# A fused four-stage kernel on one Trainium2 core: block 2's local sums taken out of the head into group 0, and each deferred block's x1 loaded in one piece

## The chip, the cores and the metric

The kernel runs on 1 core of one Trainium2 chip. The metric is the device time of the whole program in microseconds (us), lower is better. Before the change it is 701.6 us, the median of 3 runs (700.96 to 702.64). Instructions of five engines run side by side and wait for each other on semaphores: PE (TensorE), DVE (VectorE), ACT (ScalarE), POOL (GpSimd) and SP (SyncE, which here only issues DMAs).

## The reference

`x` has shape 2 x 2048 x 512 (two sequences, f32). Four residual stages follow each other:

```
x = x + L0(x)   # per sequence: scores from tanh(x W1 + b1) v, masked softmax over all positions, pooled sum / count
x = x + L1(x)   # stencil: zX*(left + right - 2y) along channels + zY*(row before + row after - 2y) + zR*y*(1-y)
x = x + L2(x)   # adapter: LayerNorm(y + relu(y Wd + bd) Wu + bu), weights picked by profile id
x = x + L3(x)   # recurrent mixer: causal EMAs (scans over time), gates (Wg, Wn1, Wtemp, Wsoma), Wout, LayerNorm
```

The output of L0's stage is called x1 below, that of L1's stage x2, that of L2's stage x3. For the stencil stage the kernel splits x2 of a block of rows into local sums (x1*(mid - zR*x1), and zX times the left and right channel neighbours), which need that block alone, and the rows before and after it, scaled by zY, which are added by DMA from a copy in DRAM (`beside_scratch`).

## The kernel before, in words

The 4096 rows are 32 chunks of 128 rows; 4 chunks make a block (512 rows), and there are 8 blocks, 0 to 3 in the first sequence, 4 to 7 in the second. Each engine has one instruction stream, written out by hand; every wait is a semaphore wait in that stream, and what stands behind it on the engine waits too.

**The head** (up to about 139 us) computes L0. PE alternates the score matmuls (L1030, L1043, L1050), the sums, the transposes of the probabilities (L1086, L1099) and `pooled(b, c)` (L1125, L1126), one chunk of x1 each; DVE finishes a chunk in `x1(b, c)` (L1513), which also frees the PSUM bank that a later `pooled` writes. Between these, PE does the adapter of block 0: `x2_transposes(0)` (L1164), `down(0)` (L1174), `up(0)` (L1184), and DVE and ACT its LayerNorm. Blocks 0 to HEAD_BLOCKS-1 = 2 get their local sums here, over whole blocks of 128 x 2048: ACT `mix_local(n)` (L742), DVE `by_local(n)` (L1519), POOL `channels(n)` (L574 to L577, into `side`, which lies in `xts[2]`), DVE `stencil(n)` (L1526). ACT `scale_beside(n)` (L756) writes zY*x1 of each block, in place for the head's blocks and into one of three `xts` slots for the others; SP `store_beside(n)` (L410) writes it to DRAM, `store_x1(n)` (L419) writes x1 of blocks 3 to 7 to `x1_scratch`. POOL then adds to x2 in place by DMAs: `add_up_bias(q)` and `add_shift(q)` (L615), `add_before(q)` (L605), `add_after(q)` (L611), each 1 MB.

**The groups** g = 0 to 7 follow, one per block: PE runs `front(g)` (N1, four times 24 matmuls of gate logits with one small matmul L1224 behind the first set), `x2_transposes(g+1)`, `soma_in`, `down(g+1)`, `up(g+1)`, `temporal(g)`, `x3_transposes(g+1)` (L1193) and `output(g)`; nearly all its matmuls are at L1129 to L1131. DVE runs for each chunk k `logits` (scan, L1647), `traces` (L1655 to L1668), `blend_traces` (L1676) and `trace_lo` (L1684), then the LayerNorm of block g+1 (L1616, L1623, L1631), `product` and `product_lo` (L1690, L1697), `x3_lo(g+1)` (L1638) and `out_apply` (L1705, L1709).

The local sums of blocks 3 to 7 are **deferred**: they are made in group q-3 and early in q-2, one chunk at a time. SP `load_late(q, c)` (L429) loads a chunk of x1 into the single buffer `late_y` once the chunk before is consumed, ACT `late_mix` (L766) writes into x2, DVE `late_by_local` (L1603) and `late_stencil` (L1609), POOL `late_channels` (L584 to L588, into `late_side`). The x2 buffers of blocks 2, 4, 6 (`x2b0`) and 3, 5, 7 (`x2b1`), the traces (`th`, `tl`) and others lie over memory that the head uses, `xb` and the `xts` slots among them: an engine that first writes there waits until the stores that read it have landed (`beside_landed`). In group 0, `trace_lo(0, 0)` waits so for block 7's store.

## Time and profile before

| what | before |
|---|---|
| median of 3 runs | 701.6 us |
| the profiled execution: its own time / its span | 702.7 us / 700.7 us |
| PE busy | 666.1 us (95%) |
| DVE busy | 526.5 us (75%) |
| ACT busy | 363.3 us (52%) |
| POOL busy | 174.2 us (25%) |
| chain that ended last | PE 79%, DVE 9%, ACT 4%, DMA 4%, SP's queue 2% |
| moved by DMA | 85.77 MB, mean 122 GB/s |

Start times are microseconds from the start of the span. "Idle before <- releaser" is how long the engine stood before the instruction and whose semaphore came last. PE's busy time counts overlapping matmuls once. The granted clock of PE is given as a share of 2.4 GHz, so 0.50 is its lower level of 1.2 GHz.

### The profile page before, as it was taken

How to read it: one execution, taken by the hardware profiler on the slowest of the kernel's cores; microseconds unless marked ns; L12 is line 12 of the kernel's file. 1: busy time of each engine (PE TensorE's matmuls, PEld its weight loads, DVE VectorE, ACT ScalarE, POOL GpSimd, SP SyncE). 2: the span in 40 equal slices, each digit the busy share in tenths (PEclk: the TensorE clock that was granted, in tenths of full speed). 3: DMA queues.
4: the chain of work that ended last, by engine and by line, in shares of the span. 5: the costliest groups of instructions: out<-in, count | busy, mean ns of one | idle time of the engine just before them, and what ended most of it. 6: DMA issues, size and time to landing. Idle time of an engine off the chain costs nothing.

```text
span 700.7 us, 8057 instructions
## 1 busy us (share of the span) xinstructions
PE 666.1 (95%) x2792; PEld 484.8 (69%) x2792; DVE 526.5 (75%) x747; ACT 363.3 (52%) x745; POOL 174.2 (25%) x259
## 2 busy tenths in 40 slices
PE   4969988989999999999999999999999999999996
PEld 1535444468577868786878687868786878687875
DVE  2676789847996888589868986887689649864955
ACT  0143366582675366536653566456635653565245
POOL 5003440110044214411451235123512210111001
PEclk9989999999999999999999999999999999999998
DMA  7996998999522661465147524742465230022001
GB/s 201 326 335 222 258 203 201 359 263 322 106 36 74 150 101 29 102 135 97 30 117 129 87 35 120 131 77 39 127 93 88 38 83 1 0 48 74 0 1 60
DMA packets 51670, 85.77 MB, mean 122 GB/s; under 512 B 8480, under 2 KB 10528, under 8 KB 51630
## 3 DMA queue, kind: packets, MB, share of 16 engines
q0 software_dynamic: 16896, 33.56, 30.1%
q1 hardware_dynamic: 31230, 51.69, 20.6%
q10 hardware_dynamic: 3504, 0.01, 0.3%
q8 instruction: 22, 0.36, 0.2%
q14 instruction: 18, 0.15, 0.1%
HBM read 63.22 MB, written 22.04 MB: 122 GB/s over the span
## 4 chain that ended last, share of the span: by engine, by line
PE 79%; DVE 9%; ACT 4%; DMA 4%; SPq 2%; issue 1%; POOLq 0%; ACTq 0%; POOL 0%; DVEq 0%
PE bank L1130 20%; PE bank L1129 20%; PE bank L1131 20%; PE bank L1184 3%; PE bank L1174 3%; PE bank L1125 3%; PE bank L1030 3%; DMA beside_scratch<-xts 2%; PE bank L1164 2%; PE bank L1193 2%; DMA xts<-in_xT 1%; SPq L410 1%; DVE xb L1513 1%; DVE x2b L1519 1%; PE bank L1224 1%
## 5 line engine op out<-in xcount | busy, mean ns | idle before, releaser
L1668 DVE TENSOR_TENSOR_SCAN tr<-alpha,carry,tr 128x512 f32<-128x512 f32 x48 | 58.8, 1267 | 0.0
L1129 PE MATMUL bank<-th,wg_l 128*128 128x512 f32 x128 | 52.0, 406 | 0.0
L1129 PE MATMUL bank<-xh,wg_l 128*128 128x512 f32 x128 | 51.9, 406 | 0.0
L1130 PE MATMUL bank<-tl,wg_h 128*128 128x512 f32 x128 | 50.5, 395 | 0.0
L1130 PE MATMUL bank<-xl,wg_h 128*128 128x512 f32 x128 | 50.5, 395 | 0.0
L1131 PE MATMUL bank<-th,wg_h 128*128 128x512 f32 x128 | 50.2, 392 | 0.0
L1131 PE MATMUL bank<-xh,wg_h 128*128 128x512 f32 x128 | 50.2, 392 | 0.0
L840 ACT ACTIVATE carry<-tr 128x2 f32<-128x2 f32 x32 | 6.6, 205 | 80.4 <-DVE tr L1668 80.3
L624 POOL TENSOR_TENSOR rs_a<-ss_a,consts 128x1 f32<-128x1 f32 x32 | 14.3, 447 | 118.7 <-ACT junk L788 118.1
L1125 PE MATMUL bank<-xb,probT 128*128 128x512 f32 x64 | 36.4, 652 | 5.5 <-DVE xb L1513 5.4
L1655 DVE SCALAR_TENSOR_TENSOR wgb<-wgb,soma 128x512 f32<-128x512 f32 x32 | 22.2, 692 | 25.4 <-ACT wgb L834 25.4
L1647 DVE TENSOR_TENSOR_SCAN wgb<-alpha,carry,bank 128x512 f32<-128x512 f32 x24 | 30.4, 1266 | 9.8 <-PE bank L1131 9.8
L858 ACT ACTIVATE wide<-bank,bias_temp 128x512 f32<-128x512 f32 x32 | 21.8, 683 | 29.6 <-PE bank L1131 29.6
L1690 DVE SCALAR_TENSOR_TENSOR wide<-wide,soma 128x512 f32<-128x512 f32 x32 | 21.3, 685 | 18.9 <-ACT wide L858 18.9
L584 POOL TENSOR_TENSOR late_side<-late_y 128x510 f32<-128x510 f32 x20 | 21.4, 1072 | 53.7 <-DMA late_y<-x_scratch 53.6
L766 ACT ACTIVATE x2b<-late_y,coef 128x512 f32<-128x512 f32 x20 | 16.2, 810 | 35.0 <-DMA late_y<-x_scratch 35.0
L1603 DVE TENSOR_TENSOR x2b<-x2b,late_y 128x512 f32<-128x512 f32 x20 | 14.7, 736 | 25.9 <-ACT x2b L766 25.8
L1709 DVE SCALAR_TENSOR_TENSOR xr<-wgb,rs_o,xr 128x512 f32<-128x512 f32 x32 | 27.7, 864 | 6.3 <-POOL rs_o L626 4.7
L1705 DVE SCALAR_TENSOR_TENSOR wgb<-bank,nmu_o,gamma_row 128x512 f32<-128x512 f32 x32 | 23.9, 746 | 9.4 <-ACT junk L874 9.2
L1513 DVE SCALAR_TENSOR_TENSOR xb<-bank,rnorm,xb 128x512 f32<-128x512 f32 x32 | 23.0, 743 | 10.5 <-PE bank L1126 10.5
L615 POOL DMA_DIRECT2D xr<-rows_scratch x10 | 13.5, 1350 | 63.3 <-PE bank L1193 52.9
L624 POOL TENSOR_TENSOR rs_o<-ss_o,consts 128x1 f32<-128x1 f32 x32 | 8.4, 262 | 83.0 <-ACT junk L874 83.0
(264 smaller groups left out, 1995.3 us busy)
## 6 DMA issues: line engine op xcount, KB each, us to landing
x2b<-beside_scratch POOLq DMA_DIRECT2D x12, 1024.0 KB, 9.2
xr<-rows_scratch POOLq DMA_DIRECT2D x10, 1024.0 KB, 10.6
xb<-in_x SPq DMA_DIRECT2D x8, 1024.0 KB, 14.2
result<-xr SPq DMA_DIRECT2D x7, 1024.0 KB, 4.2
x2b<-rows_scratch POOLq DMA_DIRECT2D x6, 1024.0 KB, 9.5
x_scratch<-xb SPq DMA_DIRECT2D x5, 1024.0 KB, 10.5
beside_scratch<-xts SPq DMA_DIRECT2D x5, 1024.0 KB, 11.5
late_y<-x_scratch SPq DMA_DIRECT2D x20, 256.0 KB, 2.9
```

What stands on the lines that cost most here:

```text
L624: po.tensor_tensor(rs[:, c:c + 1], ss[:, c:c + 1], eps, ALU.add).then_inc(chain, 1)
L858: act.activation(wide[:, k], bank[TEMP(g)[k]][:], ACT.Tanh, bias=bias_temp[:, k:k + 1], scale=0.5).then_inc(gate_act, 1)
L1125: pe.matmul(acc, probT[:, c], xb[:, b, c], start=True, stop=False)
L1129: pe.matmul(acc, wl, xh_, start=start, stop=False)
L1130: pe.matmul(acc, wh, xl_, start=False, stop=False)
L1131: return pe.matmul(acc, wh, xh_, start=False, stop=stop)
L1513: ve.scalar_tensor_tensor(xb[:, b, c], bank[POOLED(b, c)][:], rnorm[:, b, c:c + 1], xb[:, b, c], ALU.mult, ALU.add).then_inc(x1_done, 1)
L1647: ve.tensor_tensor_scan(wgb[:, k % 2], alpha[:, 0:1].broadcast_to([P, GN]), bank[CTX[k]][:], 0.0 if first else carry[:, k, 0:1], ALU.mult, ...
L1655: ve.scalar_tensor_tensor(w, w, 1.0, x3f[:, k], ALU.add, ALU.mult).then_inc(gated, 1)
L1668: ve.tensor_tensor_scan(t[:, d], alpha[:, 1 + d:2 + d].broadcast_to([P, GN]), t[:, d], 0.0 if first else carry[:, k, 1 + d:2 + d], ALU.mul ...
L1705: ve.scalar_tensor_tensor(t, bank[OUT[c]][:], nmu_o[:, c:c + 1], gamma_row[:], ALU.add, ALU.mult).then_inc(o_w, 1)
L1709: ve.scalar_tensor_tensor(xr[:, g % 2, c], t, rs_o[:, c:c + 1], xr[:, g % 2, c], ALU.mult, ALU.add).then_inc(o_done, 1)
```

## The change

1. `HEAD_BLOCKS` is 2. `mix_local(2)`, `by_local(2)`, `stencil(2)` and `channels(2)` leave the head. Block 2 is handled as the deferred ones, chunk by chunk: chunk 0 and 1 between the end of the head and group 0's first logits, 2 and 3 within group 0. Its x1 is copied by one DMA from `xb` to `x2b0` (`keep_x1`, SBUF to SBUF), and its `beside` copy goes through an `xts` slot.
2. `load_late(q)` loads the whole block (1 MB) straight into its x2 buffer instead of four chunks into `late_y`. `late_mix` writes to a separate tile `late_mixed`, `late_by_local` multiplies in place, and must now wait for POOL's `late_channels`, which reads the same chunk.
3. The `xts` slots are used in another turn, so the waits on landed stores name earlier blocks: `trace_lo(0, 0)` waits for block 6's, not block 7's.
4. On DVE `trace_lo(g, k)` for k = 0, 1 moves behind the next chunk's `logits` and `blend_traces`; the deferred stencils of chunk 3 and chunk 2 move up a place. POOL's three adding DMAs for block 2 move into group 0.

```diff
-HEAD_BLOCKS = 3
+HEAD_BLOCKS = 2
...
-                return x1_of(n) if n < HEAD_BLOCKS else as_tiles(xts[n % 3])
+                return x1_of(n) if n < HEAD_BLOCKS else as_tiles(xts[(n - HEAD_BLOCKS) % 3])
...
+                    def keep_x1(q):
+                        sp.wait_ge(x1_done, GT * (q + 1))
+                        sp.wait_ge(beside_out[0][0], 32)
+                        sp.dma_start(x2_of(q), x1_of(q)).then_inc(late_in, 16)
...
+                    def load_late(q):
+                        sp.wait_ge(x1_out[q], 16)
+                        if q == HEAD_BLOCKS + 1:
+                            beside_landed(sp, 1, 3)
                         else:
-                            sp.wait_ge(late_v, n)
-                            sp.wait_ge(late_chan, 3 * n)
-                        sp.wait_ge(x1_out[q], 16)
-                        sp.dma_start(late_y[:], x1_rows(q)[:, c]).then_inc(late_in, 16)
+                            sp.wait_ge(x3_done, GT * (q - 1))
+                        sp.dma_start(x2_of(q), x1_rows(q)).then_inc(late_in, 16)
...
+                        n, y = late_tile(q, c), x2_of(q)[:, c]
+                        po.wait_ge(late_in, 16 * (q - 1))
+                        if n:
+                            po.wait_ge(late_done, n)
+                        else:
+                            po.wait_ge(pool_mm, B * NT)
...
-                    channels(2)
                     add_before(1)
                     add_after(1)
                     for c in range(GT):
                         rstd(ln_ss, ss_a, EPSILON, rs_a, c, ln_p, ln_rs, c)
+                    late_channels(2, 0)
                     add_shift(0)
-                    add_up_bias(2)
...
+                        if g == 0:
+                            for c in range(1, GT):
+                                late_channels(2, c)
+                            add_up_bias(2)
...
-                        act.activation(x2_of(q)[:, c], late_y[:], ACT.Identity, bias=coef[:, MID, b:b + 1],
+                        act.activation(late_mixed[:], x2_of(q)[:, c], ACT.Identity, bias=coef[:, MID, b:b + 1],
...
                     act.wait_ge(x1_out[3], 16)
+                    late_mix(2, 0)
                     x3_evict(0)
+                    late_mix(2, 1)
                     scale_beside(6)
...
                         ve.wait_ge(late_u, n + 1)
-                        ve.tensor_tensor(x2_of(q)[:, c], x2_of(q)[:, c], late_y[:], ALU.mult).then_inc(late_v, 1)
+                        ve.wait_ge(late_chan, 3 * (n + 1))
+                        ve.tensor_tensor(x2_of(q)[:, c], x2_of(q)[:, c], late_mixed[:], ALU.mult).then_inc(late_v, 1)
...
                         if g == 0 and k == 0:
-                            beside_landed(ve, 1, 3)
+                            beside_landed(ve, 1, 2)
```

**VectorE at the end of the first sequence's pooling**, around the moved block. Before (L1513 is `x1`, L1519 `by_local(2)`, L1508 `sums_low(1)`, L1526 `stencil(2)`, L1500 the start of `normalise(1)`):

```order
L1513 SCALAR_TENSOR_TENSOR xb<-bank,rnorm,xb 128x512
L1519 TENSOR_TENSOR x2b<-x2b,xb 128x2048
L1513 SCALAR_TENSOR_TENSOR xb<-bank,rnorm,xb 128x512
L1508 TENSOR_TENSOR g_hl<-bank,g_hl 16x512
L1513 SCALAR_TENSOR_TENSOR xb<-bank,rnorm,xb 128x512 x2
L1526 SCALAR_TENSOR_TENSOR x2b<-xts,coef,x2b 128x2048
L1500 TENSOR_REDUCE zin<-prob 128x16
```

In the changed kernel (L1526 is now `x1`, L1521 `sums_low(1)`, L1513 `normalise(1)`):

```order
L1526 SCALAR_TENSOR_TENSOR xb<-bank,rnorm,xb 128x512 x2
L1521 TENSOR_TENSOR g_hl<-bank,g_hl 16x512
L1526 SCALAR_TENSOR_TENSOR xb<-bank,rnorm,xb 128x512 x2
L1513 TENSOR_REDUCE zin<-prob 128x16
L1514 TENSOR_TENSOR zin<-zin,zout 128x16
```

Both whole-block instructions are gone; nothing stands between the last four x1 chunks but `sums_low(1)`.

**VectorE from the end of the head into group 0.** Before (L1638 `x3_lo(0)`, L1598 the low part of Wsoma, L1647 `logits`, L1655 to L1668 `traces`, L1676 `blend_traces`, L1684 `trace_lo`):

```order
L1638 TENSOR_TENSOR xl<-soma,xh 128x512 x4
L1598 TENSOR_TENSOR ws_l<-prob,ws_h 128x2048
L1647 SCALAR_TENSOR_TENSOR wgb<-alpha,bank 128x512
...
L1668 SCALAR_TENSOR_TENSOR tr<-alpha,tr 128x512 x2
L1684 TENSOR_TENSOR tl<-tr,th 128x512
L1647 SCALAR_TENSOR_TENSOR wgb<-alpha,bank 128x512
L1676 SCALAR_TENSOR_TENSOR tr<-tr,blend_w 128x512
L1655 SCALAR_TENSOR_TENSOR wgb<-wgb,soma 128x512
```

In the changed kernel (L1617 `late_by_local`, L1622 `late_stencil`, L1652 `x3_lo`, L1611 the low part of Wsoma, L1661 `logits`, L1682 end of `traces`, L1690 `blend_traces`, L1698 `trace_lo`, L1669 start of the next `traces`):

```order
L1617 TENSOR_TENSOR x2b<-x2b,late_mixed 128x512
L1652 TENSOR_TENSOR xl<-soma,xh 128x512 x4
L1622 SCALAR_TENSOR_TENSOR x2b<-late_side,coef,x2b 128x512
L1611 TENSOR_TENSOR ws_l<-prob,ws_h 128x2048
...
L1682 SCALAR_TENSOR_TENSOR tr<-alpha,tr 128x512 x2
L1661 SCALAR_TENSOR_TENSOR wgb<-alpha,bank 128x512
L1690 SCALAR_TENSOR_TENSOR tr<-tr,blend_w 128x512
L1698 TENSOR_TENSOR tl<-tr,th 128x512
L1669 SCALAR_TENSOR_TENSOR wgb<-wgb,soma 128x512
```

Block 2's eight chunk instructions are spread over this stretch, and `trace_lo` of a chunk stands behind the next chunk's scan and blend.

**SP's queue in the head.** Before, `store_beside(1)` and `store_beside(2)` (L410), then `store_x1(3)`:

```order
L410 DMA beside_scratch<-xb 128x4x512 x2
L419 DMA x_scratch<-xb 128x4x512
L410 DMA beside_scratch<-xts 128x4x512
L414 DMA beside_scratch<-xts 1x512
L488 DMA prob<-in_wsoma 128x4x512
```

In the changed kernel `keep_x1(2)` (L424) stands between them, and block 2's store reads `xts`:

```order
L410 DMA beside_scratch<-xb 128x4x512
L424 DMA x2b<-xb 128x2048
L410 DMA beside_scratch<-xts 128x4x512
L419 DMA x_scratch<-xb 128x4x512
L410 DMA beside_scratch<-xts 128x4x512
```

The order of the rest of that queue is the same up to the first deferred load.

## Rows read from the trace of the kernel before

**Rows 1.** Windows by stage; columns: busy us (instructions) per engine, clock, DMA share, GB/s
```profile
209.00:642.00 433.00, 433.00 (x1880) 337.49 (x1879) 335.65 (x460) 240.31 (x529) 120.71 (x182) 1.00 0.42 81
...
80.00:209.00 129.00, 117.27 (x466) 72.87 (x465) 107.19 (x140) 76.18 (x121) 30.46 (x34) 0.97 0.85 219
```

**Rows 2.** Timeline of PE; columns: start us, us, engine, line, instruction [idle before <- releaser]
```profile
102.42 1.12 PE L1099 MATMUL bank<-ident,prob 128*128 128x128 f32 x8 [0.30 <-ACT probT L732]
106.92 2.04 PE L1125 MATMUL bank<-xb,probT 128*128 128x512 f32 x2 [3.38 <-DVE xb L1513]
...
110.69 1.02 PE L1125 MATMUL bank<-xb,probT 128*128 128x512 f32 x2
...
111.78 1.02 PE L1125 MATMUL bank<-xb,probT 128*128 128x512 f32 x2
...
112.88 1.04 PE L1164 MATMUL bank<-ident,xr 128*128 128x128 f32 x8
```

**Rows 3.** Windows just behind that wait (columns as in rows 1)
```profile
106.00:108.00 2.00, 1.08 (x3) 0.60 (x3) 2.00 (x3) 2.00 (x2) 0.00 (x0) 0.65 0.91 76
```

**Rows 4.** Timeline of DVE, block 2's two instructions in the head
```profile
97.89 6.06 DVE L1519 TENSOR_TENSOR x2b<-x2b,xb 128x2048 f32<-128x2048 f32 x1 [2.22 <-ACT x2b L742]
...
106.69 2.34 DVE L1526 SCALAR_TENSOR_TENSOR x2b<-xts,coef,x2b 128x2048 f32<-128x2048 f32 x1
```

**Rows 5.** Timeline of POOL, the issue of `add_after(0)`
```profile
96.89 1.28 POOL L611 DMA_DIRECT2D xr<-beside_scratch  x1 [9.38 <-DMA beside_scratch<-xb]
```

**Rows 6.** DMA issues of 96 to 97.5 us: count, KB each, us to landing
```profile
xr<-beside_scratch POOLq DMA_DIRECT2D x1, 1024.0 KB, 9.3
```

**Rows 7.** DMA issues of 161 to 162 us
```profile
x2b<-beside_scratch POOLq DMA_DIRECT2D x1, 1024.0 KB, 13.5
```

**Rows 8.** The page's DMA queues: packets, MB, share of 16 engines; q1 is SP's
```profile
q1 hardware_dynamic: 31230, 51.69, 20.6%
```

**Rows 9.** The page's costliest groups: `late_mix` (count | busy us, mean ns | idle before)
```profile
L766 ACT ACTIVATE x2b<-late_y,coef 128x512 f32<-128x512 f32 x20 | 16.2, 810 | 35.0 <-DMA late_y<-x_scratch 35.0
```

**Rows 10.** Timeline of PE in group 0
```profile
151.69 1.10 PE L1224 MATMUL bank<-nar,wn_half 128*128 128x512 f32 x2 [0.37 <-issue]
...
190.49 0.50 PE L1129 MATMUL bank<-th,wt_l 128*128 128x512 f32 x1 [1.31 <-DVE wt_l L1598]
...
206.28 0.50 PE L1129 MATMUL bank<-wo_h,xl 128*128 128x512 f32 x1 [0.25 <-DVE xl L1697]
```

**Rows 11.** Timeline of DVE in group 0
```profile
171.36 0.69 DVE L1684 TENSOR_TENSOR tl<-tr,th 128x512 fp32r<-128x512 f32 x1 [3.92 <-DMA beside_scratch<-xts]
171.97 1.21 DVE L1647 TENSOR_TENSOR_SCAN wgb<-alpha,bank 128x512 f32<-128x512 f32 x1
...
174.21 0.69 DVE L1655 SCALAR_TENSOR_TENSOR wgb<-wgb,soma 128x512 f32<-128x512 f32 x1 [0.38 <-ACT wgb L834]
...
179.04 1.21 DVE L1647 TENSOR_TENSOR_SCAN wgb<-alpha,bank 128x512 f32<-128x512 f32 x1
...
207.03 0.69 DVE L1603 TENSOR_TENSOR x2b<-x2b,late_y 128x512 f32<-128x512 f32 x1
207.76 0.75 DVE L1609 SCALAR_TENSOR_TENSOR x2b<-late_side,coef,x2b 128x512 f32<-128x512 f32 x1
```

**Rows 12.** Timeline of DVE, `ln_apply` in group 1 and in group 5 (no `late_channels` beside it)
```profile
266.06 2.85 DVE L1631 SCALAR_TENSOR_TENSOR xr<-tr,rs_a,x2b 128x512 f32<-128x512 f32 x3
...
544.21 2.07 DVE L1631 SCALAR_TENSOR_TENSOR xr<-tr,rs_a,x2b 128x512 f32<-128x512 f32 x3
```

**Rows 13.** Timeline of ACT in group 1
```profile
275.21 0.80 ACT L766 ACTIVATE x2b<-late_y,coef 128x512 f32<-128x512 f32 x1
```

**Rows 14.** Timeline of PE, the first matmul of `front(2)`
```profile
285.83 0.39 PE L1129 MATMUL bank<-xh,wn_l 128*128 128x512 f32 x1
```

**Rows 15.** Timeline of POOL, the last `rstd` of group 0
```profile
223.84 0.89 POOL L626 TENSOR_TENSOR rs_o<-rs_o,consts 128x1 f32<-128x1 f32 x1
```

**Rows 16.** The chain of waits, `x2_transposes(2)`
```profile
242.25 1.75 PE bank L1164 x16
```

More of the change, by code:

```diff
@@ L481, in _ @@
                     store_beside(1)
+                    keep_x1(2)
                     store_beside(2)
@@ L506, in _ @@
                         if g + 3 < GROUPS:
-                            for c in range(GT):
-                                load_late(g + 3, c)
+                            load_late(g + 3)
                         sp.wait_ge(o_done, GT * g + GT)
@@ L654, in _ @@
                             add_shift(g + 1)
+                        if g == 0:
+                            add_before(2)
                         if late:
@@ L968, in _ @@
                         mod_affine(g)
+                        if g == 0:
+                            late_mix(2, 2)
                         keep_traces(g, 0)
@@ L1011, in _ @@
                         for c in range(GT):
-                            if late and c == 3:
+                            if late and c == 2:
                                 late_mix(g + 3, 2)
@@ L1779, in _ @@
                     zero_edge(0)
+                    late_by_local(2, 0)
                     x3_lo(0)
+                    late_stencil(2, 0)
                     weight2_low(1, ws_h[:], ws_l[:], ws_st)
+                    late_by_local(2, 1)
+                    late_stencil(2, 1)
                     assert n["p"] == S_PARAMS, n["p"]
@@ L1794, in _ @@
                         traces(g, 0)
+                        if g == 0:
+                            late_by_local(2, 2)
+                            late_stencil(2, 2)
                         logits(g, 1)
@@ L1810, in _ @@
                             weight2_low(2, wt_h[:], wt_l[:], wt_st[:])
+                            late_by_local(2, 3)
+                            late_stencil(2, 3)
                             weight2_low(3, wo_h[:], wo_l[:], wo_st[:])
@@ L1838, in _ @@
                         for c in range(GT):
-                            if late and c == 3:
+                            if late and c == 2:
                                 late_by_local(g + 3, 2)
```

52 lines of the change are left out of this document (20 added, 32 removed).

## The prediction

> **What bounds the kernel now.** I read the windows by stage first, then PE's timeline, then the engines that PE waits for. From 209 to 642 us PE is busy in every microsecond of 433, DVE in 335.65 [rows 1]: nothing that DVE, ACT, POOL or a DMA does there can shorten the kernel, it can only add to it. From 80 to 209 us PE is busy 117.27 of 129 us [rows 1]. The 11.7 us that it stands there are all that this change can win, since it removes no matmul. The largest of these gaps is in the head: PE ends its transposes at 102.42 + 1.12 = 103.54 and starts the next `pooled` at 106.92, released by DVE's x1 chunk [rows 2]. DVE is late because `by_local(2)` takes 6.06 us after a wait of 2.22 for ACT's `mix_local(2)`, and 2.34 us more go to `stencil(2)` [rows 4]. The smaller gaps are in group 0, where the path runs through DVE: PE waits 1.31 us for the low part of Wtemp and 0.25 for `product_lo` [rows 10], and DVE itself had stood 3.92 us before `trace_lo(0, 0)` for block 7's store [rows 11]. After 206.28 PE does not stand again until the last group, whose tail the change leaves alone. So I count how much earlier the matmul of 206.28 starts, and take that as the gain.
>
> **The head.** 8.3 us (6.06 + 2.22) leave DVE between two x1 chunks, so x1(0, 15) is ready before PE's transposes end; ACT and PE pass those among themselves and are not changed. PE can go on at 103.54 instead of 106.92, which is 3.4 us. Behind the wait the granted clock is 0.65 and the four `pooled` take 112.88 - 106.92 = 5.96 us [rows 2, 3]; at full clock one takes 111.78 - 110.69 = 1.09, four 4.36 [rows 2]. Without the wait I count full clock, 1.6 us more. `x2_transposes(0)` could then start at 107.9 instead of 112.88, 5.0 us earlier.
> But it also needs `add_after(0)`, a DMA issued at 96.89 and landed 9.3 us later, at 106.2 [rows 5, 6]. New beside it is `keep_x1(2)`, 1 MB on SP's queue as soon as chunk 11 is done, behind `store_beside(1)`. SP's queue takes 20.6% of 700.7 us for 51.69 MB [rows 8], 2.8 us of all 16 engines per MB. If the two share the engines, `add_after(0)` lands at 109.0. Bounds: no delay at all (107.9, PE's own time), and the slowest such transfer in a crowded stretch, 13.5 us [rows 7], so 110.4. I take 109.0: **3.9 us earlier** (2.5 to 5.0). The rest of the head is then the same chain, `down(0)`, `up(0)`, LayerNorm, `x3_transposes(0)`, moved as it stands. DVE's `normalise(1)` and the weights before x1(1, 0) end in time, as `stencil(2)` is gone. The wait of the first `y_sum` on `keep_x1` and on block 2's store costs nothing: both are asked for some 10 us before it.
> The Trainium skill ("DMA: Bandwidth & Descriptors", section on queues, rings and completion order) says that each DMA engine takes its queues in turn, packet by packet, which is the sharing I assume; if the queues did not share, the head would gain 5.0 and the sum 1.1 more.
>
> **From the head's end to the first logits.** ACT gets two `late_mix` (0.81 us each [rows 9]) before the table load and the Gelu that PE's small matmul at 151.69 waits for; PE stands 0.37 there already [rows 10], so ACT is the path. The second counts whole, 0.8. The first is released by the last `pooled`, while PE still does its first four transposes, so I count 0.2 of it (0 to 0.8). Together **+1.0** (0.8 to 1.6). On DVE `late_by_local(2, 0)` now waits for POOL's `late_channels(2, 0)` and holds `x3_lo(0)` behind it by about 1 us, but its four chunks are paced by ACT and the last is not late. `late_stencil(2, 0)` and the pair of chunk 1 fall into DVE's waits for ACT.
>
> **Group 0 on DVE.** Each pair is 0.69 + 0.75 us, 1.3 from start to start [rows 11]. The pair of chunk 2 stands between `traces(0)` and `logits(1)`, on the path: **+1.3**. Then `logits(2)` follows `traces(1)` at once: the wait of 3.92 goes and with it `trace_lo(0)`, 0.6 (171.36 to 171.97): **-4.5**. Block 6's store, the one now asked for, was issued some 10 us ahead of block 7's. `trace_lo` moves behind the blend, where DVE stood 0.38 for ACT in each chunk [rows 11]. One period (171.97 to 179.04) shrinks from 7.1 to 6.7: **-0.4**; the next one gives back **+0.2**, since it takes in a `trace_lo` more. What is late next is ACT's `weight_hi` of Wtemp before the last sigmoid, within 0.1 us by the same count.
> For the moved POOL work I add **+0.4** (0 to 0.8). `ln_apply` of three chunks takes 2.85 us where `late_channels` runs beside it and 2.07 where it does not [rows 12], so one such overlap costs DVE 0.8. Of the four new ones three fall into DVE's waits; the one of chunk 3 meets `blend_traces(0)`.
> The Trainium skill ("SBUF — State Buffer", the points on the shared port pair) speaks against this change: GpSimd and a VectorE instruction with two SBUF inputs exclude each other for the whole instruction. By it the same move could cost its full length four times; the difference of 0.8 agrees in kind.
> The pair of chunk 3 stands behind Wtemp's low part: **+1.3** for the LayerNorm and the products.
>
> **Sum at the matmul of 206.28.** By DVE: -3.9 + 1.0 + 1.3 - 4.5 - 0.4 + 0.2 + 0.4 + 1.3 = **-4.6**. PE's own way: -3.9 + 1.0, less the 1.31 for Wtemp, less its short waits around the products, about 0.8 of which only 0.25 has a row [rows 10]: -5.0. The later one decides, -4.6. Ends: -2.5 + 1.6 with the port at 0.8 gives about -2.2; -5.0 + 0.8 with the port at 0 gives -6.3.
>
> **Later groups: nothing, under cover of PE.** `add_up_bias(2)`, `add_before(2)` and `add_after(2)` (1 MB each) move to group 0. The last is issued after the rstd of 223.84 + 0.89 [rows 15] and, at 9.3 to 13.5 us, lands at 234 to 238.2; PE wants it at 242.25 [rows 16], and both move together. Cover: 4 us. `load_late(4)` to `load_late(7)` wait for the block's `ln_apply`, 266.06 + 2.85 = 268.9 in group 1 [rows 12]; ACT wants the data at 275.21 [rows 13], so a landing within 6.3 us delays nothing. Behind it stand ACT's `x3_evict` and POOL's `add_shift`, which PE needs at 285.83 and later [rows 14]. The old waits of ACT and POOL for `late_y` go, off the path. The changed DVE order does not reach PE.
>
> The profiled execution took 702.7 us, 2.0 over its span of 700.7 and 1.1 over the median of 701.6. It would become 698.1; on the median, 701.6 - 4.6 = **697.0 us**. Its own range is 695.3 to 699.4. About 0.2% (1.4 us) is what a measurement of this kernel can tell from no change.
>
> **Rivals.**
> A, *the head's gain stays with the DMAs.* `keep_x1` and `add_before(1)`, which POOL now issues earlier, hold up `add_after(0)` until 112.9, 16 us after its issue. For it: the engines are loaded at 0.85 over the whole stretch [rows 1]. Against: 13.5 us is the slowest other such row [rows 7]. Then -4.6 + 3.9 = -0.7: 700.9. Chance 0.09.
> B, *slower: the 1 MB load becomes the wait in each group.* It is asked for only when the old block leaves its buffer. ACT stands for it ahead of `x3_evict`; PE's `front` reads the last of that 2 us after 285.83, ACT and DVE end it at about 281.4, so 6.5 us of slack lie behind the 6.3. It decides from a landing of 12.8 us on. At 15 us it costs 2.2 us in each of four groups, 8.8 in all: 705.8. For it: the same megabyte took 13.5 us in a crowded stretch [rows 7]; against: DMA is busy only 0.42 from 209 us on [rows 1]. Chance 0.04.
> C, *slower: POOL locks DVE out.* By the rule above all four `late_channels` of block 2 lie on the path, each about 1.9 us of POOL time: 7.6 instead of 0.4, so +2.6: 704.2. Against: rows 12 show 0.8, and DVE has waits there. Chance 0.03.
> D, *more than counted.* With block 2's adding DMAs gone from 141 to 185 us the weights and stores land earlier, and PE wins back gaps in the head that I left: up to 8 of the 11.7 us, 693.6. Chance 0.06.
> Forecast 0.78.
>
> **Numbers.** The range takes the forecast's ends and part of A and D: 694.6 to 700.2. Faster by over 0.2%: forecast and D, 0.84. Within 0.2%: A, 0.09. Slower: B and C, 0.07.
>
> **What would show it.** PE's wait of 3.38 us for x1 is gone, `x2_transposes(0)` starts near 109 with a short wait for a DMA before it, and the clock is 1.00 behind it. The wait at the small matmul of group 0 grows from 0.37 to about 1.4. DVE has no wait for `beside_scratch`, PE none for Wtemp; the matmul of 206.28 starts near 201.7. From there to the last group PE is busy throughout, the period between groups unchanged. I am wrong if `x2_transposes(0)` starts at 112 or later (A), if PE stands in `front` of groups 2 to 5 (B), or if DVE's short instructions in group 0 are drawn out (C).

## The result, and the profile after

The changed kernel took **697.18 us** (median of 4 runs, 696.72 to 697.44), the kernel before beside it 701.56 (700.96 to 702.64): ratio 0.9935, 95% interval 0.9918 to 0.9952. A second set of runs (E5) gave 697.12 against 703.07, ratio 0.9917 (0.9900 to 0.9935). The forecast was 697.0. The gain is 4.4 us in the first set and 5.95 in the second. The kernel before varies more than the changed one: 17 runs of it beside E1 to E4 lie between 700.6 and 705.8 us, the 6 of E5 between 696.6 and 697.9, and the first set had 4 of its faster ones.

The profiled execution took 697.24 us, its span is 695.4. I go through its rows in the order of the prediction. Windows by stage (columns as in [rows 1]; the last line answers to [rows 3]):

```profile
80.00:209.00 129.00, 120.12 (x488) 76.70 (x488) 108.51 (x151) 82.13 (x135) 32.97 (x46) 0.99 0.82 223
203.50:636.50 433.00, 433.00 (x1879) 336.96 (x1878) 341.59 (x460) 240.50 (x530) 123.49 (x183) 1.00 0.44 85
106.00:108.00 2.00, 2.00 (x7) 0.97 (x6) 2.00 (x2) 2.00 (x2) 0.00 (x0) 1.00 1.13 210
```

PE is busy 2.9 us more from 80 to 209 us, still in every microsecond of the 433 behind, and the granted clock from 106 to 108 us is 1.00 where it was 0.65. Timeline of PE, the end of the head (answers to [rows 2]):

```profile
102.75 1.12 PE L1112 MATMUL bank<-ident,prob 128*128 128x128 f32 x8 [0.29 <-ACT probT L744]
103.71 1.02 PE L1138 MATMUL bank<-xb,probT 128*128 128x512 f32 x2
...
108.06 1.03 PE L1177 MATMUL bank<-ident,xr 128*128 128x128 f32 x8
```

The wait of 3.38 us is gone, and `x2_transposes(0)` starts with no wait. `add_after(0)`, the DMA it needs, was issued at 96.11 (POOL's timeline) and took 10.4 us. So it landed at 106.5, 1.5 us before PE asked. Timeline of PE in group 0 (answers to [rows 10]) and in the last group:

```profile
147.49 1.10 PE L1237 MATMUL bank<-nar,wn_half 128*128 128x512 f32 x2 [1.10 <-issue]
...
196.81 1.97 PE L1206 MATMUL bank<-ident,xr 128*128 128x128 f32 x16 [0.71 <-DVE xr L1645]
200.05 0.50 PE L1142 MATMUL bank<-wo_h,xl 128*128 128x512 f32 x1 [0.22 <-DVE xl L1711]
201.25 0.50 PE L1142 MATMUL bank<-wo_h,xl 128*128 128x512 f32 x1 [0.25 <-DVE xl L1711]
...
678.15 0.50 PE L1142 MATMUL bank<-wo_h,tl 128*128 128x512 f32 x1 [0.90 <-DVE tl L1711]
```

The small matmul waits 1.10 instead of 0.37, the wait for Wtemp is gone, and a new one of 0.71 stands before `x3_transposes(1)`. The matmul of 206.28 now starts at 201.25. In the last group PE stands 0.90 us; before it was 1.25. Timeline of DVE in group 0 (answers to [rows 11]), and in a fence of its own the instruction of ACT's timeline behind which DVE's 0.92 lies:

```profile
156.70 0.67 DVE L1617 TENSOR_TENSOR x2b<-x2b,late_mixed 128x512 f32<-128x512 f32 x1
157.40 0.75 DVE L1622 SCALAR_TENSOR_TENSOR x2b<-late_side,coef,x2b 128x512 f32<-128x512 f32 x1
158.07 1.21 DVE L1661 TENSOR_TENSOR_SCAN wgb<-alpha,bank 128x512 f32<-128x512 f32 x1
159.20 0.72 DVE L1690 SCALAR_TENSOR_TENSOR tr<-tr,blend_w 128x512 f32<-128x512 f32 x1
...
164.56 1.19 DVE L1661 TENSOR_TENSOR_SCAN wgb<-alpha,bank 128x512 f32<-128x512 f32 x1
...
171.16 1.19 DVE L1661 TENSOR_TENSOR_SCAN wgb<-alpha,bank 128x512 f32<-128x512 f32 x1
172.62 0.75 DVE L1690 SCALAR_TENSOR_TENSOR tr<-tr,blend_w 128x512 f32<-128x512 f32 x1 [0.27 <-ACT carry L849]
...
179.71 0.75 DVE L1690 SCALAR_TENSOR_TENSOR tr<-tr,blend_w 128x512 f32<-128x512 f32 x1 [0.92 <-ACT carry L849]
181.16 0.69 DVE L1698 TENSOR_TENSOR tl<-tr,th 128x512 fp32r<-128x512 f32 x1 [0.70 <-ACT th L857]
181.77 2.28 DVE L1611 TENSOR_TENSOR wt_l<-wt_l_f,wt_h 128x2048 fp32r<-128x2048 f32 x1
183.97 0.68 DVE L1617 TENSOR_TENSOR x2b<-x2b,late_mixed 128x512 f32<-128x512 f32 x1
```

```profile
178.81 0.69 ACT L788 ACTIVATE nar<-bank,db_cols 128x512 f32<-128x512 f32 x1 [2.75 <-PE bank L1187]
```

No wait for `beside_scratch` is left. `logits(0, 2)` starts at 164.56, before at 171.97. But from `logits(0, 3)` to Wtemp's low part it is 10.6 us now (171.16 to 181.77) and was 9.1 (179.04 [rows 11] to 188.15). DVE now waits for ACT, which stands 2.75 us for PE's `down` product in `relu(1)`, ahead of `keep_traces(0, 3)`.

**Two stretches.** When PE does the last eight transposes of `prob` differs from run to run by some 2 us (it is 101.38 in one trace of this text and 103.59 in another), which is more than some of the effects below. So I compare two stretches of each trace: *front*, from those transposes to the small matmul of group 0, and *rest*, from there to the end of the span. In two profiles of the same kernel they agree within 0.12 us (the changed kernel twice, E8 twice). That does not hold for the front of the kernels with the old head (before, E4, E6, E9): it is 49.3 to 50.9 us there, though nothing in the head differs between them, so a front read from one trace of the kernel before is uncertain by more than 1 us (see E9).

| kernel | front | rest | time |
|---|---|---|---|
| before | 49.27 | 549.01 | 701.56 |
| changed | 44.74 | 547.91 | 697.18 |
| E1 old trace order | 44.77 | 547.91 | 696.76 |
| E2 wait for block 7 | 44.75 | 547.75 | 696.88 |
| E3 head only | 43.75 | 548.97 | 697.63 |
| E4 whole-block load | 49.91 | 548.23 | 702.20 |
| E5 changed, second set | 44.75 | 547.89 | 697.12 |
| E6 adds in group 0 | 49.43 | 548.54 | 702.58 |
| E7 one mix later | 44.04 | 547.81 | 696.77 |
| E8 and `relu(1)` later | 44.04 | 546.77 | 695.62 |
| E9 = E4 and E6 | 50.90 | 546.60 | 700.26 |
| E10 = E8, last tile later | 44.05 | 545.76 | 695.57 |
| E11 = E8, channels later | 44.04 | 547.58 | 694.95 |
| E12 = E8 again | 44.04 | 546.65 | 695.39 |

Beside E1 to E4 the kernel before took 703.25, beside E5 to E8 703.07, E9 and E10 703.14, E11 and E12 702.63; ratios below are to those. The change itself is -4.5 in the front and -1.1 in the rest; of this 1.1, 0.8 lies before the matmul of 201.25 and 0.3 behind it, about the 0.35 of the last group.

### The profile page after: what moved, and what is told of

Its sections match the earlier page's. It is cut to its first block, busy times and chain, and to the rows that moved or that the text cites. A ratio compares the mean times of both kernels' runs of the same rounds, so it can differ in the third digit from the quotient of the medians.

```text
span 695.4 us, 8056 instructions
## 1 busy us (share of the span) xinstructions
PE 664.6 (96%) x2792; PEld 484.4 (70%) x2792; DVE 528.4 (76%) x753; ACT 364.0 (52%) x748; POOL 176.5 (25%) x268
## 3 DMA queue, kind: packets, MB, share of 16 engines
q0 software_dynamic: 16896, 33.56, 29.7%
q1 hardware_dynamic: 31134, 52.74, 21.2%
## 4 chain that ended last, share of the span: by engine, by line
PE 86%; DVE 7%; ACT 4%; issue 1%; DMA 1%; SPq 0%; POOLq 0%; ACTq 0%; POOL 0%; DVEq 0%
PE bank L1142 22%; PE bank L1143 22%; PE bank L1144 21%; PE bank L1187 4%; PE bank L1043 4%; PE bank L1197 3%; PE bank L1138 3%; PE bank L1177 2%; PE bank L1206 2%; PE bank L1237 1%; DMA v_sb<-in_v 1%; DVE tr L1637 1%; DVE xb L1526 1%; PE bank L1139 1%; PE bank L1112 1%
## 5 line engine op out<-in xcount | busy, mean ns | idle before, releaser
L1682 DVE TENSOR_TENSOR_SCAN tr<-alpha,carry,tr 128x512 f32<-128x512 f32 x48 | 58.9, 1267 | 0.0
L630 POOL TENSOR_TENSOR rs_a<-ss_a,consts 128x1 f32<-128x1 f32 x32 | 15.9, 498 | 121.6 <-ACT junk L797 121.2
L1669 DVE SCALAR_TENSOR_TENSOR wgb<-wgb,soma 128x512 f32<-128x512 f32 x32 | 22.0, 687 | 30.2 <-ACT wgb L843 30.2
L590 POOL TENSOR_TENSOR late_side<-x2b 128x510 f32<-128x510 f32 x24 | 27.0, 1126 | 60.0 <-DMA x2b<-x_scratch 26.9
L830 ACT ACTIVATE mod<-bank,bias_n 64x512 f32<-64x512 f32 x32 | 21.9, 683 | 37.6 <-PE bank L1237 37.0
L1704 DVE SCALAR_TENSOR_TENSOR wide<-wide,soma 128x512 f32<-128x512 f32 x32 | 24.0, 766 | 23.1 <-ACT wide L867 23.1
L1661 DVE TENSOR_TENSOR_SCAN wgb<-alpha,carry,bank 128x512 f32<-128x512 f32 x24 | 30.2, 1259 | 9.8 <-PE bank L1144 9.8
L1723 DVE SCALAR_TENSOR_TENSOR xr<-wgb,rs_o,xr 128x512 f32<-128x512 f32 x32 | 31.6, 989 | 4.4 <-POOL rs_o L632 3.9
L1690 DVE SCALAR_TENSOR_TENSOR tr<-tr,blend_w 128x512 f32<-128x512 f32 x32 | 23.4, 731 | 13.9 <-ACT carry L849 13.9
L1526 DVE SCALAR_TENSOR_TENSOR xb<-bank,rnorm,xb 128x512 f32<-128x512 f32 x32 | 23.0, 744 | 11.7 <-PE bank L1139 11.7
L1719 DVE SCALAR_TENSOR_TENSOR wgb<-bank,nmu_o,gamma_row 128x512 f32<-128x512 f32 x32 | 23.9, 747 | 10.4 <-ACT junk L883 10.2
L630 POOL TENSOR_TENSOR rs_o<-ss_o,consts 128x1 f32<-128x1 f32 x32 | 6.7, 208 | 92.8 <-ACT junk L883 92.3
L1197 PE MATMUL bank<-uw,nar 128*128 128x512 f32 x64 | 29.0, 594 | 0.0
```

Source lines behind the costliest of these rows:

```text
L590: po.tensor_tensor(late_side[:, 1:E - 1], y[:, 0:E - 2], y[:, 2:E], ALU.add)\
L1197: pe.matmul(bank[UP(q)[c]][:], z[:, chunk(c)], uw[:, b], start=True, stop=True)\
L1526: ve.scalar_tensor_tensor(xb[:, b, c], bank[POOLED(b, c)][:], rnorm[:, b, c:c + 1], xb[:, b, c], ALU.mult, ALU.add).then_inc(x1_done, 1)
L1661: ve.tensor_tensor_scan(wgb[:, k % 2], alpha[:, 0:1].broadcast_to([P, GN]), bank[CTX[k]][:], 0.0 if first else carry[:, k, 0:1], ALU.mult, ...
L1682: ve.tensor_tensor_scan(t[:, d], alpha[:, 1 + d:2 + d].broadcast_to([P, GN]), t[:, d], 0.0 if first else carry[:, k, 1 + d:2 + d], ALU.mul ...
L1723: ve.scalar_tensor_tensor(xr[:, g % 2, c], t, rs_o[:, c:c + 1], xr[:, g % 2, c], ALU.mult, ALU.add).then_inc(o_done, 1)
```

## The experiments

**E1. The traces in the old order.** The changed kernel, with DVE's two `trace_lo` back in front of the next `logits`.

```diff
-                        logits(g, 2)
-                        blend_traces(g, 1)
                         trace_lo(g, 0)
+                        logits(g, 2)
+                        blend_traces(g, 1)
                         traces(g, 2)
-                        logits(g, 3)
-                        blend_traces(g, 2)
                         trace_lo(g, 1)
+                        logits(g, 3)
+                        blend_traces(g, 2)
```

> The changed kernel with one part undone: on VectorE trace_lo(g, k) for k = 0, 1 stands before the next chunk's logits again. My theory (the path of group 0 runs through VectorE, and trace_lo behind the blend fills a wait of 0.38 us for ScalarE): each of the two trace_lo costs 0.6 us on the path less the 0.4 that the wait gave, so the kernel is slower than the changed one by 0.4 to 0.9 us, 697.6 to 698.1. Rival (the new order is what removed the wait for the store, by asking for it later): the wait of VectorE for beside_scratch is back, 2 us and more, 699 and more. Second rival (the order does nothing, since ScalarE is next on the path): within 0.2 us of the changed kernel.

Measured 696.76 (ratio 0.9914, 0.9896 to 0.9932), both stretches as in the changed kernel. DVE's timeline has three waits of 0.38 for ACT's gate again, and the one behind `relu(1)` shrinks:

```profile
179.62 0.75 DVE L1690 SCALAR_TENSOR_TENSOR tr<-tr,blend_w 128x512 f32<-128x512 f32 x1 [0.34 <-ACT carry L849]
```

DVE's reordering is worth nothing, as the second rival of the expectation had it: ACT decides when Wtemp's low part can start.

**E2. The old wait back.** The changed kernel, where DVE's `trace_lo(0, 0)` also waits for block 7's store.

```diff
                             beside_landed(ve, 1, 2)
+                            beside_landed(ve, 1, 3)
```

> The changed kernel with one wait added: trace_lo(0, 0) waits for block 7's store too, as before. In the changed kernel SP has seen that store land before 159.9 us, where it issues load_late(3), while trace_lo(0, 0) runs at 166.3. Theory A (the store now lands early because block 2's adding DMAs left the stretch; the new turn of the slots is worth nothing by itself): same time as the changed kernel, within 0.2 us. Theory B (my prediction's reading: asking for block 6 is what removed the wait): VectorE waits again, 1 to 4 us, 698 to 701.

Measured 696.88 (0.9913, 0.9889 to 0.9938), and DVE has no wait for a DMA. So the removed wait of 3.92 us does not need the earlier store: in the changed kernel block 7's has landed too (SP, which also waits for it, goes on at 159.88). That asking for block 6's would have been enough by itself, with the adding DMAs where they were, is not refuted by this. In the kernel before, that store was issued at 145.92 and landed 13.5 us later, at 159.4, and ACT, whose first `trace_hi` waits for it, ran at 162.99, while DVE began its wait at 167.44. From the DMA issues and ACT's timeline of the kernel before:

```profile
beside_scratch<-xts SPq DMA_DIRECT2D x1, 1024.0 KB, 13.5
```

```profile
162.99 0.62 ACT L848 ACTIVATE th<-tr 128x512 fp32r<-128x512 f32 x1
```

No run had the new turn of the slots alone.

**E3. The head alone.** The kernel before, with `by_local(2)` and `stencil(2)` on 32 of 2048 columns and `channels(2)` on 10 of 512 in each chunk; the rest of block 2's local sum is left out of the result. ACT's `mix_local(2)` stays whole.

```diff
-                        po.tensor_tensor(side[:, :, 1:E - 1], xg[:, :, 0:E - 2], xg[:, :, 2:E], ALU.add)\
+                        w = 10 if n == 2 else E
+                        po.tensor_tensor(side[:, :, 1:w - 1], xg[:, :, 0:w - 2], xg[:, :, 2:w], ALU.add)\
...
-                        s = flat(local_of(n))
+                        w = 32 if n == 2 else GT * E
+                        s = flat(local_of(n))[:, 0:w]
...
-                        ve.tensor_tensor(s, s, flat(x1_of(n)), ALU.mult).then_inc(mix_v, 1)
+                        ve.tensor_tensor(s, s, flat(x1_of(n))[:, 0:w], ALU.mult).then_inc(mix_v, 1)
...
```

> The kernel before, with VectorE's and GpSimd's part of block 2's local sums left out but for 32 of 2048 columns (so block 2's result lacks them); everything else is as before, its adding DMAs and the wait for block 7's store too. Theory A (the whole chain moves along): PE goes on at about 103.6, x2_transposes(0) starts near 108, the wait of 3.9 us at trace_lo(0, 0) stays as long as it is, gain 4.8 to 5.0, 696.7. Theory B (the store's landing is set by the crowded DMA queue and not by when it is issued): the wait grows from 3.9 to 6 to 9 us, and the gain is 1 to 3 us, 698.6 to 700.6.

Measured 697.63 (0.9929, 0.9905 to 0.9953). Timelines of DVE and PE:

```profile
98.24 0.19 DVE L1521 TENSOR_TENSOR x2b<-x2b,xb 128x32 f32<-128x32 f32 x1 [2.23 <-ACT x2b L743]
...
166.16 0.69 DVE L1687 TENSOR_TENSOR tl<-tr,th 128x512 fp32r<-128x512 f32 x1 [3.86 <-DMA beside_scratch<-xts]
```

```profile
146.53 1.10 PE L1225 MATMUL bank<-nar,wn_half 128*128 128x512 f32 x2 [0.39 <-issue]
...
185.30 0.50 PE L1130 MATMUL bank<-th,wt_l 128*128 128x512 f32 x1 [1.25 <-DVE wt_l L1601]
```

The front is 5.5 shorter and the rest as before, down to the wait of 3.86. This alone is within 0.1 us of what the whole change gives in the trace (43.75 + 548.97 = 592.72 against 592.65): all that the change does behind the head comes to nothing, 1.0 lost in the front and 1.1 won in the rest. By the medians E3 is 0.5 us slower (697.63 against 697.12 in E5).

**E4. Whole-block loads alone.** The kernel before with three blocks in the head, and one load of 1 MB for each deferred block.

```diff
-                            for c in range(GT):
-                                load_late(g + 3, c)
+                            load_late(g + 3)
...
-                        sp.dma_start(late_y[:], x1_rows(q)[:, c]).then_inc(late_in, 16)
+                        sp.dma_start(x2_of(q), x1_rows(q)).then_inc(late_in, 16)
...
```

> The kernel before, with three head blocks still, but each deferred block (3 to 7) loaded by one DMA straight into its x2 buffer, late_mixed in place of late_y, and late_by_local waiting for late_channels. My theory (all of it lies under PE's cover in groups 1 to 7): no difference from the kernel before, within 0.7 us. Rival B of the prediction (the load, asked for only when the old block leaves its buffer, becomes a wait in each group): slower by up to 2 us per group, and PE's timeline shows waits in front of groups 2 to 5. Other rival (the chunk loads had cost something): faster by 1 us or more.

Measured 702.20 (0.9985, 0.9966 to 1.0003): no difference that the times can tell, and no new wait in a later group. PE's wait for Wtemp is 0.94 us instead of 1.31, and the one in the last group 0.90 instead of 1.25. The latter is 0.90 or 0.91 in every kernel with this load and 1.25 in the three without it (before, E3, E6), so these 0.35 us of the change belong to its second part; the rows do not say why.

**E6. Only block 2's adding DMAs moved.** The kernel before, with POOL's three accumulating DMAs in group 0.

```diff
-                    add_up_bias(2)
...
-                        if g + 2 < GROUPS:
+                        if g == 0:
+                            po.wait_ge(beside_out[1][3], 32)
+                            add_up_bias(2)
+                        elif g + 2 < GROUPS:
...
+                        if g == 0:
+                            add_before(2)
...
+                        if g == 0:
+                            add_after(2)
```

> The kernel before with one thing changed: POOL issues the three accumulating DMAs of block 2 (add_up_bias, add_before, add_after) in group 0, as the changed kernel does, and not in the head. Block 2's local sum stays in the head. Theory A (those DMAs crowd the stretch in which block 7's store is issued, so the store lands late and VectorE waits 3.9 us for it at trace_lo): without them the store has landed before it is asked for, the 3.9 us wait is below 0.5, the result of trace_lo comes 3 to 4 us earlier, and the time falls by what TensorE still waited for group 0's last products, 1.2 to 2.5 us, so 701.0 where the kernel before is at 703.2. Theory B (the store is late by itself, by its place behind the 16 late tiles' loads on SyncE or by its size): the wait stays between 3 and 4 us and the time within 0.5 us of the kernel before. The head's wait of 3.4 us at the third step's transposes stays under both.

Measured 702.58 (0.9996, 0.9980 to 1.0013). Timelines of DVE, PE and ACT:

```profile
168.13 0.67 DVE L1690 TENSOR_TENSOR tl<-tr,th 128x512 fp32r<-128x512 f32 x1
...
184.69 0.75 DVE L1682 SCALAR_TENSOR_TENSOR tr<-tr,blend_w 128x512 f32<-128x512 f32 x1 [1.76 <-ACT carry L846]
```

```profile
224.82 1.10 PE L1230 MATMUL bank<-nar,wn_half 128*128 128x512 f32 x2 [1.32 <-ACT nar L818]
```

```profile
216.09 0.82 ACT L772 ACTIVATE x2b<-late_y,coef 128x512 f32<-128x512 f32 x1 [5.74 <-DMA late_y<-x_scratch]
```

Theory A had the cause right: moving these DMAs is enough to end the wait of 3.9 us at `trace_lo`. It had the worth wrong (1.2 to 2.5 us). DVE gives 1.76 of it back to ACT, and the adds now run beside the loads of block 3's tiles (6.2 us to landing in the median of four, before 2.7), for which ACT stands 5.74 us ahead of group 1's Gelu (3.65 before). PE pays 1.32.

**E9. E4 and E6 together.** Both diffs above.

> The kernel before with two parts of the change that brought nothing each by itself: the three accumulating DMAs of block 2 in group 0 (702.6 against 703.1 alone), and one whole-block load for each deferred block in place of four loads by tile (702.2 alone). Block 2's local sum stays in the head. Theory A (with the adds alone, the loads of block 3's tiles, 9.8 us to landing beside them where they took 2.7, held ScalarE 5.7 us and TensorE 1.3 us at the small matmul of group 1, and this ate the gain of the removed 3.9 us wait; a load that was asked for tens of us before cannot do so): together they gain what neither does, TensorE has no wait of 1.3 us in group 1, and the time is 1.0 to 2.0 below the kernel before, 701.1 to 702.1. Theory B (the two do not act on each other): the time is the sum of both, 0 to 1.0 below, and the wait at the small matmul of group 1 stays above 1 us.

Measured 700.26 (0.9959, 0.9942 to 0.9976). In group 1's small matmul (223.51) PE has no wait. The rest is 2.4 us shorter, where E4 and E6 have 0.8 and 0.5: 1.2 more than their sum, about the 1.32 that PE paid in E6. So in the traces the two parts of the change need each other: the adds moved away free the store, and the load in one piece, issued at 161.48 and first read by ACT at 205.12, does not mind the adds. The medians alone do not show this: the intervals of E4, E6 and E9 are too wide to tell 2.9 from the sum of the other two, 1.3. The front is 1.6 longer than before. DVE's `by_local(2)` takes 6.84 us here (6.72 in E4, 6.22 in E6, 6.06 before [rows 4]). In all four traces it ends 2.15 to 2.16 us after POOL's whole-block instruction of `channels(2)`, which stands behind the issue of `add_after(0)` and that DMA's wait for a store: the later POOL comes, the longer `by_local(2)` takes. Up to `x2_transposes(0)` E9 is 2.0 us longer than before, 0.8 of it from there; the rest goes with the clock, which was 0.50 over the 6 us from 106 to 112 here and 0.72 over the same stretch before. So the trace shows 0.8 for the whole where the medians show 2.9; the twelve runs lie between 697.83 and 702.54, and the profiled one is among the slower. The size stays open, the direction not: the interval excludes 1.

**E5, E7, E8. The changed kernel again, and two steps of ACT moved.** E7 puts `late_mix(2, 1)` and its DVE pair behind the first Gelu; E8 also puts `relu(1)` behind `keep_traces(0, 3)`.

```diff
-                    late_mix(2, 1)
                     scale_beside(6)
...
                         n1_gelu(g)
+                        if g == 0:
+                            late_mix(2, 1)
...
-                        if adapted:
+                        if adapted and g:
                             relu(g + 1)
                         keep_traces(g, 3)
                         trace_hi(g, 3)
+                        if g == 0:
+                            relu(1)
...
```

> The changed kernel itself, beside the two variants built from it, on the same chip: 696.8 to 697.3, ratio to the kernel before 0.991 to 0.994. It gives the time against which the two variants are read, nothing else.

> The changed kernel with one tile's share of group 0's late mixing put later: ScalarE's late_mix(2, 1) behind n1_gelu(0), and VectorE's late_by_local(2, 1) and late_stencil(2, 1) behind logits(0, 0), where it waits for ScalarE anyway (4.10 us at its traces). Theory A (the 0.8 us instruction in front of the Gelu is what the small matmul's wait of 1.10 us consists of): that wait falls to 0.3 to 0.5 us, all of group 0 behind it comes 0.7 earlier, and the time is 0.5 to 0.8 below the changed kernel. Theory B (the 0.8 us only moves to ScalarE's next step, keep_traces or the evictions behind it, which is on the same path): the small matmul's wait falls, the products of group 0 come at the same time as in the changed kernel, no difference (within 0.2).

> The last variant with one more step: in group 0 ScalarE does keep_traces(0, 3) and trace_hi(0, 3) before relu(1), for which it stands 2.75 us until TensorE's product is there. Theory A (the waits of VectorE for ScalarE's traces, 0.27 and 0.92 us, are on the path to the low weights): both are gone, the products of group 0 come 0.7 to 1.1 earlier than in the last variant, and the time is 0.6 to 1.0 below it, 1.2 to 1.7 below the changed kernel, 695.5 where that is at 697.0. Theory B (relu(1) later makes TensorE wait for the up product of group 1, which then is late for its own transposes): the gain is given back, no difference to the last variant, or up to 1 us slower than it.

Measured 697.12, 696.77 and 695.62 (0.9917, 0.9909 and 0.9892 with 0.9874 to 0.9910). In E7 the small matmul's wait falls from 1.11 to 0.40 and the front by 0.71: the `late_mix` before the Gelu cost nearly all of its 0.8. In E8 the rest falls by 1.04, since ACT's `keep_traces` no longer stands behind PE; DVE's wait of 0.92 is gone, the one of 0.27 stays. In the traces both went by theory A. By the medians E7 is 0.35 us below E5, less than the 0.5 to 0.8 that A gave, with ranges that overlap; E8's runs (694.28 to 696.10) all lie below E5's.

**E10. The last tile of block 2 later.** E8 with the tile's three steps behind the last product, and the adds behind them.

```diff
-                            late_mix(2, 3)
...
                         product_hi(g, KE - 1)
-                        if late:
+                        if g == 0:
+                            late_mix(2, 3)
+                        elif late:
                             late_mix(g + 3, 0)
...
```

> The version of e8 with the last tile of block 2 mixed later: late_mix(2, 3), late_by_local(2, 3) and late_stencil(2, 3) behind the last product of group 0 in place of between the two low weights, and block 2's three adding DMAs behind it (add_up_bias near 203 us in place of 185). Theory A (the pair of 1.37 us is on VectorE's path to the products): VectorE's sums of y start 1.3 earlier, the products of group 0 with them, and the time is 1.0 to 1.3 below e8, 694.3 to 694.6, if the adds, 203 + 9.8 + 12 + 9.4, land by 234.8, when TensorE asks for block 2. Theory B (they land later than that; the adds are the next bound): the front gains 1.3, but TensorE waits 1 to 4 us at the transposes of block 2, and the time is the same as e8 or up to 3 us above it. I hold B for a little likelier, 55 to 45.

Measured 695.57 (0.9904, 0.9882 to 0.9926), as E8, though the rest is 1.0 shorter in the trace; the six runs (694.30 to 696.92) are too far apart to tell. Neither theory held. Timeline of DVE:

```profile
184.27 2.29 DVE L1620 TENSOR_TENSOR wo_l<-wo_l_f,wo_h 128x2048 fp32r<-128x2048 f32 x1 [1.45 <-ACT wo_h L907]
...
192.82 2.08 DVE L1654 SCALAR_TENSOR_TENSOR xr<-tr,rs_a,xr 128x512 f32<-128x512 f32 x3
```

Where the pair stood, DVE now waits 1.45 us for ACT's high part of Wout: A is wrong, the pair cost nothing there (from Wtemp's low part to Wout's it is 3.74 us, and 3.58 in E8). B is wrong too, the last add landed at 225.69 + 9.1 = 234.8 and PE began at 235.22 without a wait, with 0.4 us to spare. What came earlier was `ln_apply`: 2.08 us, where E8 has 2.85. The only thing beside it that had gone was POOL's `late_channels(3, 0)`.

**E11, E12. That tile of POOL by itself, and E8 again.** E8 with block 3's first tile later on POOL, ACT and DVE.

```diff
-                            if late:
+                            if late and g:
                                 late_channels(g + 3, 0)
                             add_shift(g + 1)
+                            if g == 0:
+                                late_channels(3, 0)
...
```

> The version of e8 with one tile later: POOL's late_channels(3, 0), which ran beside VectorE's ln_apply of group 1, behind add_shift(1); late_mix, late_by_local and late_stencil of that tile behind x3's evictions and low parts. The tiles of block 2 stay where e8 has them. Theory A (in e10 the only gain was that VectorE's three ln_apply took 2.08 us instead of 2.85 once POOL had nothing beside them): here they take 2.1 too, the products of group 0 come 0.8 earlier than in e8, and the span is 693.3 to 693.6 where e8 has 694.3. Theory B (in e10 it was the moved tile of block 2 that made room): ln_apply stays at 2.8 and the span at 694.3.

> The version of e8 once more, beside e11, since the two are to be compared at less than 1 us: 695.2 to 696.1, span 694.0 to 694.6, ln_apply 2.8 us.

Measured 694.95 (0.9892, 0.9871 to 0.9912) and 695.39 (0.9893, 0.9874 to 0.9912). Timelines of DVE, E11 and then E12:

```profile
190.83 2.07 DVE L1652 SCALAR_TENSOR_TENSOR xr<-tr,rs_a,xr 128x512 f32<-128x512 f32 x3
...
196.67 2.96 DVE L1718 TENSOR_TENSOR xl<-wide,xh 128x512 fp32r<-128x512 f32 x2
```

```profile
192.37 2.85 DVE L1648 SCALAR_TENSOR_TENSOR xr<-tr,rs_a,xr 128x512 f32<-128x512 f32 x3
...
198.98 1.47 DVE L1714 TENSOR_TENSOR xl<-wide,xh 128x512 fp32r<-128x512 f32 x2
```

Timelines of POOL and PE in E11, the new place of that tile and who pays:

```profile
196.94 1.53 POOL L590 TENSOR_TENSOR late_side<-x2b 128x510 f32<-128x510 f32 x1
197.95 1.16 POOL L592 TENSOR_SCALAR late_side<-x2b 128x1 f32<-128x1 f32 x1
198.14 1.54 POOL L594 TENSOR_SCALAR late_side<-x2b 128x1 f32<-128x1 f32 x1
```

```profile
199.08 0.50 PE L1149 MATMUL bank<-wo_h,xl 128*128 128x512 f32 x1 [1.89 <-DVE xl L1718]
```

Theory A held for `ln_apply`, and the expectation for the time failed: the same POOL work now lies beside `product_lo`, whose last two take 2.96 us instead of 1.47, on the path. PE waits 1.89, and the rest is 0.9 longer than in E12. The median is nevertheless 0.4 lower. In the trace that is no gain of the edit: PE's transposes of `prob` happened to end 1.5 us earlier there. The five runs of each overlap (694.7 to 696.2 against 695.3 to 696.1) and tell nothing. **E8, 695.6 and 695.4 in two sets, beats both kernels**, by 1.5 us of the changed one.

## Why the prediction was right, and where not

The forecast of the time held, by errors against each other: the head gave 1.25 us more than I counted, the way to the first logits cost 0.4 less, and group 0 gave 0.9 less. That it fell within 0.2 us is luck as well: I forecast a gain of 4.6, the spans of the two traces differ by 5.3, and the two sets of runs by 4.4 and 5.95.

- **Head, -3.9.** From PE's last transposes of `prob` to `x2_transposes(0)` it was 10.46 us (102.42 to 112.88 [rows 2]) and is 5.31 (102.75 to 108.06): -5.15. Wait and clock went as said, and E3 shows that the head carries the whole gain. The term that was mis-sized is the DMA beside: I let `keep_x1` cost `add_after(0)` 2.8 us. Its landing took 1.1 longer (9.3 [rows 6] to 10.4), `add_before(1)` beside it included, it was issued 0.8 earlier, and PE never saw it. I also read `by_local(2)` as 6.06 us of work. The same instruction takes 2.28 for block 0; the other 3.8 us went with POOL's `channels(2)` beside it (last section). The sum does not change by this, since both leave the head, but moving POOL's instruction alone might have ended PE's wait of 3.38. Rival A is out. (My bound for it, 13.5 us as the slowest adding DMA, was no bound: `add_up_bias(2)`, issued at 141.59 in the kernel before, took 20.0.) On packet-wise sharing of the engines ("DMA: Bandwidth & Descriptors", queues, rings and completion order, in the Trainium skill) this says little: from 94 to 100 us the packets of the adding queue took 74.3% of the engines' time and those of SP's 34.9%, so both ran, at less than the cost I had summed.
- **Up to the first logits, +1.0.** Measured 1.0 against E3 (front 44.74 and 43.75), 0.7 of it the second `late_mix` (E7). Against the kernel before it is 0.6: from `x2_transposes(0)` to the small matmul 38.81 us (112.88 to 151.69) and 39.43 (108.06 to 147.49).
- **Pairs of chunk 2 and 3, +1.3 each.** 1.37 (156.70 to 158.07) and 1.38 (183.97 to 185.35), as said. But E10 shows that the second was worth nothing: ACT's high part of Wout would have been late by as much.
- **The store wait, -4.5.** It went, and there are two reasons, of which I gave one. I put it down to asking for block 6's store; by the rows under E2 that store had landed in time before, so this may well be enough. But E2 asks for block 7's and does not wait, and E6 leaves the order alone, moves the adding DMAs, and the wait is gone: these DMAs had made the store late. Rival D named these DMAs, but for a gain at the weights and stores that PE would feel.
- **Period -0.4, then +0.2.** The first is -0.47 (6.60 against 7.07). The second failed: +1.5. I wrote that what is late next would be ACT's `weight_hi`, within 0.1 us. It is ACT's `relu(1)`, which stands 2.75 us for PE's product ahead of `keep_traces(0, 3)`. E1 shows that the order of DVE then does not matter, E8 that 1.0 us lies there.
- **POOL port, +0.4.** Nothing at `blend_traces(0)`: 0.72 us, its length elsewhere. Beside POOL's `late_channels(2, 3)` (158.30 to 159.34) stood mainly DVE's scan, which reads one operand from PSUM.
- **Sum.** From the small matmul to the one of 206.28 it was 54.59 us and is 53.76: -0.8, where my terms of group 0 make -1.7. With the front's -4.5 and the run's start 0.3 later that is 201.25, -5.0 instead of -4.6.
- **Later groups, nothing.** `add_after(2)` landed at 225.1, PE asked at 237.06. `load_late(4)` landed in 5.6 us and ACT's `late_mix(4, 0)` started at 270.79 without a wait for it: rival B is out, by E4 too.
- **Rival C** is out as a time, but the mechanism is there; E10 and E11 show it at 0.8 and 1.5 us, and the head of the kernel before at 3.8.

## What to carry to other kernels

A wait that an edit removes is worth only the distance to what is late next, and that is often another engine's place in its own order: read what that engine stood for just before (here 2.75 us in `relu`), and move that. Before an instruction's time is counted as its work, look for the same instruction elsewhere in the trace (here 2.28 us against 6.06) and for what ran beside it. When a DMA wait goes, put the old wait back by itself and the old traffic back by itself before saying which of the two did it. And with a start that varies by more than the effect, compare stretches between two fixed instructions of the trace, not only medians.
